# Expert pairs and accumulating transfers at other steps of a pass, in a fused attention and mixture-of-experts kernel

## The reference, cut to what matters

```python
x = x + window_attention(group_norm(x))     # 8 heads, shifted windows of 64 tokens, relative bias
t = t + banded_attention(layer_norm(t))     # 4 heads, 128 tokens, band of 32
t = t + experts(layer_norm(t))              # 8 experts, the best 2 of each token

probs = softmax(xf @ gate_w + gate_b)
top2_vals, top2_idx = top_k(probs, 2)       # cw[token, expert] = its probability
for w1, bb1, w2, bb2, we in experts:
    h = gelu(xf @ w1 + bb1)                 # 128 -> 256
    acc = acc + we[:, None] * (h @ w2 + bb2)
```

## Time and profile before

| | us |
|---|---|
| median of 3 runs | 3056.23 |
| lowest and highest | 3048.73, 3058.16 |
| the profiled execution's own time | 3051.38 |
| its span, first to last instruction | 3049.6 |
| mean granted TensorE clock | 0.891 |

### The profile page before, as it was taken

One profiled execution on the slowest core, in us unless ns is written; L12 is line 12 of the kernel. 1 busy time (PEld: TensorE's weight loads), 2 busy tenths in 40 slices (PEclk: granted clock), 3 DMA queues, 4 the chain that ended last, 5 costly groups with the idle time before them and its releaser, 6 DMA issues. The chain is left out here.

```text
span 3049.6 us, 72894 instructions
## 1 busy us (share of the span) xinstructions
PE 2417.9 (79%) x26418; PEld 1716.6 (56%) x26418; DVE 1998.0 (66%) x5670; ACT 1786.3 (59%) x3430; POOL 1897.7 (62%) x1569
## 2 busy tenths in 40 slices
PE   6898888888888888888888888888888888765650
PEld 3465556566556666565556666565566666553440
DVE  3588876777677777776776776777776777662110
ACT  3666666666666666666666666666666666542220
POOL 0224455766666666766666667766666667776666
PEclk8999989999999999989999999999999999877775
DMA  2011122333333333323333333333333323335442
GB/s 77 16 34 37 48 71 55 81 67 70 71 74 74 77 76 63 81 62 74 70 74 74 77 65 76 80 63 75 70 74 74 77 56 71 82 62 141 89 82 26
DMA packets 247793, 210.77 MB, mean 69 GB/s; under 512 B 35260, under 2 KB 204360, under 8 KB 247248
## 3 DMA queue, kind: packets, MB, share of 16 engines
q0 software_dynamic: 94144, 69.54, 16.1%
q1 hardware_dynamic: 153296, 136.58, 15.9%
HBM read 119.73 MB, written 90.77 MB: 69 GB/s over the span
## 5 line engine op out<-in xcount | busy, mean ns | idle before, releaser
L1157 POOL DMA_INDIRECT out_dram<-yo,back_to x540 | 855.3, 1584 | 228.2 <-issue 174.4
L1133 POOL TENSOR_TENSOR s_sb_a<-s_sb_a,mx_a 128x512 f32<-128x512 f32 x256 | 282.4, 1103 | 771.1 <-DVE mx_a L1508 770.8
L1140 POOL DMA_INDIRECT x_sorted<-xn_c,place_i x512 | 515.3, 1006 | 138.9 <-issue 133.4
L1500 DVE TENSOR_TENSOR s_sb_a<-bank_s,bias_a 128x512 f32<-128x512 f32 x256 | 176.0, 687 | 308.4 <-PE bank_s L625 251.4
L1133 POOL TENSOR_TENSOR s_sb_b<-s_sb_b,mx_b 128x512 f32<-128x512 f32 x256 | 289.2, 1130 | 6.9 <-DVE mx_b L1508 6.9
L759 PE MATMUL bank_m<-wk_e,hid 128*128 128x128 f32 x1840 | 282.0, 327 | 0.9 <-ACT hid L1015 0.9
L759 PEld LDWEIGHTS bank_m<-wk_e,hid 128*128 128x128 f32 x1840 | 279.9, 244 | 1.7 <-issue 1.7
L752 PE MATMUL bank_m<-xe,wk_e 128*128 128x512 f32 x460 | 231.4, 628 | 34.4 <-ACT hid L1015 25.8
L686 PE MATMUL bank_to<-k_consts,p_sb_b 128*128 128x128 f32 x1024 | 182.7, 305 | 88.1 <-ACT pt_sb_a L979 76.7
L984 ACT ACTIVATE p_sb_a<-s_sb_a 128x512 f32<-128x512 f32 x256 | 160.5, 627 | 149.8 <-POOL s_sb_a L1133 149.8
L979 ACT ACTIVATE pt_sb_b<-bank_to 128x512 f32<-128x512 f32 x256 | 152.6, 596 | 155.4 <-PE bank_to L686 154.8
(11 more groups left out here) (230 smaller groups left out, 5761.9 us busy)
## 6 DMA issues: line engine op xcount, KB each, us to landing
wk_e<-in_w_experts_dram SPq DMA_DIRECT2D x127, 321.0 KB, 3.3
xs<-x_sorted SPq DMA_DIRECT2D x127, 260.0 KB, 2.8
xin<-in_x_dram SPq DMA_DIRECT2D x128, 112.0 KB
x_res<-in_x_dram SPq DMA_DIRECT2D x256, 56.0 KB
out_dram<-t SPq DMA_DIRECT2D x256, 56.0 KB
out_dram<-yo,back_to POOLq DMA_INDIRECT x540, 3.4
x_sorted<-xn_c,place_i POOLq DMA_INDIRECT x512
x_res<-in_x_dram SPq DMA_DIRECT2D x256, 8.0 KB
```

Of the source, the lines that this page charges most:

```text
L1133: pool.tensor_tensor(s[:, :, :], s[:, :, :], m[:, :, None].to_broadcast(shape), ALU.subtract).then_inc(s_sub[w], 1)
L1140: pool.indirect_dma_start(out=x_sorted.ap(), out_offset=bass.IndirectOffsetOnAxis(ap=place_i[:, d % 2, TILES * choice + t:TILES * choice + ...
L1157: pool.indirect_dma_start(out=out, out_offset=bass.IndirectOffsetOnAxis(ap=back_to[:, q % IDS, j:j + 1], axis=0), in_=yo[:, q % YO, j, :], ...
L1500: tt(s_sb[0][:, :, :].rearrange("p (r h) n -> p r (h n)", h=2), scores, bias_a[:, kind, :, :].rearrange("p (r h) n -> p r (h n)", h=2), AL ...
```

## The change

Slot 0's `into`, `mid` and `back` move from steps 1, 2 and 3 to steps 3, 4 and 5. Slot 0 may take a batch four passes old, as slot 1 does, instead of five. SyncE loads both slots' pairs of a pass one after the other, behind `spill(c, 1)` of the same pass. GpSimd's adds get other steps: slot 0 in steps 6 and 7 and in steps 0, 1, 1, 1, 2, 2 of the next pass, slot 1 in steps 3, 3, 3, 4, 4, 4, 5, 5 of the next pass. There are four `yo` buffers instead of three.

```diff
--- before.py
+++ after.py
@@ -39,12 +39,12 @@
 REGION = IMAGES * TOKENS + SLOTS
 SPARE = E * SLOTS
 BUFFER = E * REGION + SPARE
-IDS, YO = 8, 3
+IDS, YO = 8, 4
 FREE_PASSES = 1
 TABLES = 3
 SLOTS_PER_PASS = 2
 HOME, SHARE, ROW_W = D, D + 1, D + 2
-BACK_AT = ((4, 4, 4, 4, 5, 6, 7, 8), (9, 9, 9, 9, 10, 10, 10, 10))
+BACK_AT = ((6, 7, 8, 9, 9, 9, 10, 10), (11, 11, 11, 12, 12, 12, 13, 13))
 OUT_ROWS = (4, 5, 6, 7, 0, 1, 2, 3)
 B1_AT = 2 * HID
 B2_AT = B1_AT + CH
@@ -176,7 +176,7 @@
     for i in range(PASSES):
         here = [None] * SLOTS_PER_PASS
         for n in range(SLOTS_PER_PASS):
-            if i >= pairs[u].batch + (5 if n == 0 else 4) and i < PASSES - FREE_PASSES:
+            if i >= pairs[u].batch + 4 and i < PASSES - FREE_PASSES:
                 here[n] = u
                 u += 1
         slots.append(here)
@@ -404,9 +404,9 @@
             def slot(j, n):
                 return pairs[slots[j][n]] if 0 <= j < PASSES and slots[j][n] is not None else None
 
-            into = slot(i, 0) if t == 1 else slot(i, 1) if t == 6 else None
-            mid = slot(i, 0) if t == 2 else slot(i, 1) if t == 7 else None
-            back = slot(i, 0) if t == 3 else slot(i - 1, 1) if t == 0 else None
+            into = slot(i, 0) if t == 3 else slot(i, 1) if t == 6 else None
+            mid = slot(i, 0) if t == 4 else slot(i, 1) if t == 7 else None
+            back = slot(i, 0) if t == 5 else slot(i - 1, 1) if t == 0 else None
             return into, mid, back
 
         first_slots = min(i for i, here in enumerate(slots) if here != [None] * SLOTS_PER_PASS)
@@ -518,13 +518,11 @@
                     load_image(f + 1)
                 if on(c):
                     spill(c, 1)
-                if here[1] is not None:
-                    load_pair(sp, here[1])
+                for u in here:
+                    if u is not None:
+                        load_pair(sp, u)
                 if on(a):
                     load_residual(a, 0)
-                following = slots[i + 1][0] if i + 1 < PASSES else None
-                if following is not None:
-                    load_pair(sp, following)
                 if on(c):
                     spill(c, 0)
 
@@ -860,7 +858,7 @@
                 if tiled(nb - 1):
                     weighted_values_b(nb - 1)
 
-                if t == 1:
+                if t == 3:
                     read_slots()
                 if tiled(n):
                     transposed_probs(0, n)
@@ -1103,7 +1101,7 @@
                     squares(f, 1)
                 if t == 0 and on(b):
                     layer_rstd(ln_b, b, 1, mv_b, rs_b)
-                if t == 1 and into is not None:
+                if t == 3 and into is not None:
                     slots_copy(into, bank_m)
                 if mid_next is not None:
                     act.preload_act_table_set(GELU_SET)
```

## The result

| | before | after |
|---|---|---|
| median, us | 3054.06 (4 runs) | 2849.36 (4 runs) |
| lowest and highest | 3048.73, 3058.16 | 2842.63, 2857.7 |
| ratio, 95% interval | | 0.9332 [0.9301, 0.9363] |
| the profiled execution's own time | 3051.38 | 2852.25 |
| its span | 3049.6 | 2850.5 |

The account below looks back on a forecast made before the run. No engine is full; the order of waits inside a step bounds the kernel. Passes of 77.5 instead of 85.9 us gain 210 us, pass 6 +2.4, tail -12: 2831.8 us, plus 4.9 for the median, 2836 us; range 2795 to 2870.

Parts of the forecast that it names:

- The tail: Adds left after the passes: one pair less there, sure gain three adds (5.6 us), at most 19.4 us; 12 us taken.
- Steps 1 to 3: Without most of slot 0's work, they take pass 6's lengths: 9.6, 6.8 and 8.0 us.
- The landing wait of step 1: GpSimd waits 2.2 us for a transfer between two tiles; adds end at 11.6 us, just when due: costs nothing.
- the rival with both waits uncovered: Landing waits in steps 1 and 4 cost 4.4 us a pass, 2946 us; chance 0.22 shared with the clock rival's slowdown.
- its sign, `below_max` over 2.2 us into step 2: GpSimd's subtraction, due about 2.0 us into step 2, starting over 2.2 us in would show the forecast wrong.
- Step 4's wait: GpSimd's landing wait in step 4: adds end at 11.6 us and have until 14.0, so it costs nothing.
- Steps 4 and 5: mid fills idle time in step 4, 12.0 us (+0.2); back and a later logarithm make step 5 11.0 us (+1.9).
- the estimated 2.8 us: Step 4 would be this much longer if ScalarE's two table loads each had a drain; some 70 us over the program.
- Step 6: Starts with ScalarE's list 0.3 us behind, adding 0.3 us to the pass.
- the third rival: GpSimd's adds block VectorE in steps 2 and 3: 7.9 us a pass, 197 us, 3033 us; chance 0.03.
- the first rival: TensorE's clock: half clock in step 4 gives 2911 us (0.22 with landing waits); otherwise pass under 76, 2775 us.
- The slower rival: Slot 0 stands serially in steps 4 and 5's chain: 13.5 us a pass instead of 10.8, 3106 us; chance 0.05.

Follow-up runs that it names:

- e5: The changed kernel with slot 1 of pass 33 left empty, so as many pairs are placed as before the change: 2841.68 us, ratio 0.9301 to the kernel before.
- e12: e8 with slot 1 of pass 33 left empty, the same edit as in e5: 2818.02 us, ratio 0.9234 to the kernel before.
- e4: The changed kernel with one add of each slot set one step earlier, so tiles never meet inside a step: 2844.36 us, ratio 0.9327 to the kernel before.
- e8: The changed kernel with adds in other steps (slot 0: 6, 7, 7, 0, 1, 1, 2, 2; slot 1: 3, 3, 3, 3, 4, 4, 4, 5): 2816.03 us.
- e13: e9 with one add of slot 0 moved from step 0 to step 1, so two tiles meet there: 2840.71 us, ratio 0.932 to the kernel before.
- e3: The changed kernel with one of slot 1's two adds moved from step 5 to step 4: 2840.17 us, ratio 0.9319 to the kernel before.
- e9: e8 with the extra matmul of e7 in step 1: 2776.92 us, ratio 0.9096 to the kernel before.
- e6: The changed kernel with slot 0's into, mid and back in steps 2, 3 and 4: 3075.66 us, ratio 1.0062 to the kernel before.
- e7: The changed kernel with one unread matmul of 512 columns added in step 1 ahead of the gate's matmuls: 2881.39 us, ratio 0.9444 to the kernel before.

## Why the prediction came out as it did

In spans, the gain of 199.1 us is: start of pass 7 from 488.1 to 490.6, -2.5 (predicted -2.4, by luck: the passes up to 5 lost 3.7 us, and pass 6, said to be 2.4 us longer, was 1.2 us shorter); passes 7 to 30, +192.9 (24 x 8.4 = 201.6); pass 31 to the end, +8.7 (8.4 + 12 = 20.4). The median lies 2.9 us under the profiled execution, and not 4.9 above as I took from before. Of the 20 us missed between the profiled executions, 8.7 are in passes 7 to 30 and 11.7 behind them; the median's place beside the profiled execution, 7.8 us lower than assumed, took part of that back, and 13 us remain.

**The tail was mis-sized: 12 us in the prediction, nothing measured.** "The sure gain is three adds, 5.6 us" was wrong as a gain. The count was right: 154 adds were left at pass 31's start before, 151 after. But the three lie among the 42 and 39 adds ahead of the attention's last step, where GpSimd is not what bounds; behind that step, where it is, 112 remain in both, and `e5` and `e12` show the pair to be worth nothing. From pass 31's start to that step 167.0 us go by instead of 179.9, which is more than the 8.4 us predicted for pass 31; behind it 324.2 us instead of 320.0, and why is open.

**Steps 1 to 3** were taken from pass 6 and came out 0.3, 0.6 and 0.4 us longer than 9.6, 6.8 and 8.0. The landing wait of step 1 was costed at nothing, with the remark that it is just met at 11.6 us. In pass 18 it ended at 11.7 us and was met. In the fourteen passes with a shorter step 1 it was not, or it was met only in name: `below_max` started on time but right behind an add, and VectorE's L1268 took over 1 us more. `e4` and `e8`, where tiles do not meet there, have steps 2 and 3 at 6.9 and 8.1 us, and `e13` brings the price back. I took one value for the length of a step that has three (8.4, 9.2 to 9.7 and 10.8 us, the longer the more of it is at half clock), and the wait was covered only in the longest. "Just met" was costed at nothing without a reason. The size is about 0.9 us a pass (7.42 + 8.41 less `e8`'s 6.86 + 8.09), against 4.4 for the rival with both waits uncovered; its sign, `below_max` over 2.2 us into step 2, came in three of the 24 passes. Step 4's wait costs nothing, as was said: `below_max` of step 5 is on time. Even a late `below_max` in step 4 itself (3.8 us in `e4`) hides behind the gelus.

**Steps 4 and 5** were said to take 12.0 and 11.0 us and take 11.5 and 10.5. The mechanism was right: `mid` fills the idle time of both engines, the second table load starts 5.5 us into step 4 (1386.77), and the logarithm is what is late in step 5, by 1.4 us instead of 1.9. The Trainium skill (ScalarE: Activation LUTs, section What ACT_TABLE_LOAD costs) gives a drain beside the load; again 1.28 us of load show, with the next exponential 0.01 us behind it (1388.06), so the estimated 2.8 us did not come.

**Step 6** was said to be 0.3 us longer and is 1.2 us longer. The second add of step 5 puts `below_max` directly behind it, and VectorE's copy waits for it; this term was not in the sum, though VectorE blocked by GpSimd was, in the third rival, for the wrong instructions: the subtractions do it, not the adds. Against the sum it does not show, since steps 6, 7 and 0 together take 30.1 us and the prediction has 75.1 - 45.3 + 0.3 = 30.1 for them, step 6 of pass 6 having been 8.3 us long itself. In `e3`, without it, the three take 29.3 us.

**The clock** went the better way of the first rival, but in part: 8.0 us a pass at half clock against 14.8. In step 3 it fell from 5.8 to 1.1 and in step 4 from 4.0 to nothing, and in step 1 it rose from 3.4 to 4.55. The prediction has no term of its own for this. It took pass 6 as the base, which is itself at 0.82 in step 1 and 0.71 in step 4, and allowed for step 4's clock alone; step 4 is at full clock now. With step 1's half clock gone too and the adds fitted to it, the pass is `e9`'s 75.4 us, the rival's "under 76".

**How near the sum came is in part luck.** Steps 1 to 3 missed 1.3 us of price, steps 4 and 5 had 1.0 us too much, and the two nearly cancel in 77.5 against 77.9.

**The slower rival** named the right danger, a serial chain with half clock behind it, for the wrong places: steps 3 to 5 take slot 0 in without it, and steps 2 to 4 (`e6`, where the loads come late as well) do not. Its 3106 us is counted from the profiled execution, and by the median it would be 4.9 us more.

## What to carry to other kernels

A stage that already runs without the work you want to place is a good first measurement of what the work costs: the whole sum rested on one pass with an empty slot, and it held within 0.4 us of 77.9, with errors of 1.3 and 1.0 us that nearly cancel. That pass had only four adds in it, so it said nothing of what a full list on GpSimd costs. Where an engine works off a list that is only due at the next step, moving the stage and moving that list are one change: each half alone lost 3.2% and 1.4%, both gained 6.7%, and with the list fitted again and one matmul added 9.0%. "Just met" in a sum is a price that is paid wherever the step in front is shorter than the one value taken for it, and the next gain (full clock in step 1) is what uncovers it.

## What the runs showed of the hardware

- A four-column float32 copy by VectorE took 1.57 us instead of 0.24 when it began during GpSimd's two subtractions of 128x512 and these ran right behind an add, and up to 2.67 us elsewhere in the program. Another operation of four columns (L1268) took 2.22 us instead of 0.24 in step 1 of `e4`, and 1.85 instead of 0.23 in step 2 of pass 9. Each ended when the second subtraction did.
- GpSimd's indirect transfers beside VectorE did not lengthen its work (6.63 us busy in step 2 with five GpSimd instructions, 6.65 with three).
- A GpSimd subtraction recorded at 1.04 us takes 1.1 to 1.7 us by the record when it follows an add directly (1.36 in step 6 of pass 18, 1.63 in `e4`).
- The stretch at half clock moved with the waits and did not vanish by itself: 4.55 us in step 1 after the change, 6.8 us in `e4` with steps 2 and 3 shorter, 3.9 us in step 3 in `e7`, where step 1 had 1.3. One matmul of 512 columns ahead of the gate's matmuls of eight columns, with GpSimd's wait out of step 1, left 1.0 us a pass of it. What exactly the throttle answers to was not separated.
